# A decoder's two mixtures of experts with gate and input products in three fp16 passes

## The chip, the core and the metric

The kernel runs on one core of a Trainium2 chip. A core has a matrix engine (TensorE, in the trace PE, its weight loads PEld), VectorE (DVE), ScalarE (ACT), GpSimd (POOL), and SyncE (SP), which here only issues DMAs; each takes its instructions in order, and they meet at semaphores. The matrix engine reads from SBUF and writes to PSUM banks of 128 x 512 fp32. The metric is the device time of one execution in microseconds (us), median of several.

## The reference, cut to what matters

Two decoder layers over 1024 tokens of width 128. The change touches three of their six blocks.

```
# layer 0, mixture: 160 experts of inner width 64, 8 per token
probs  = sigmoid(x @ router.T + bias);  combine = 2.5 * top8(probs) / sum        # (T, 160)
h1     = silu(einsum('th,eih->eti', x, w_gate)) * combine.T[:, :, None]
out    = einsum('eti,ehi->th', h1, w_down) + silu(x @ w_gate_shared.T) @ w_down_shared.T
# layer 1, state space: in_proj, 4-tap convolution, silu, x_proj -> dt, B, C; softplus(dt);
#   16 states: h = exp(delta*A)*h + delta*B*u, y = sum C*h;  gate by silu(z), out_proj
# layer 1, mixture: 8 experts of inner width 512, 2 per token, at each of three linear maps
def moe_linear(x, router, w):  return sum_e top2_softmax(x @ router.T)[:, e] * (x @ w[e].T)
out = moe_linear(silu(moe_linear(x, rg, w_gate)) * moe_linear(x, ru, w_up), rd, w_down)
```

Inputs, weights and output are fp32.

## The kernel before

The six blocks are stages that run one after the other. Every instruction stands in an order written out by hand, engine by engine.

**First mixture** (moe0_stage, tiles f_, 971 to 1270 us). Two experts make a pair, so that their 2 x 64 inner columns fill 128 partitions: 80 pairs. The tokens are taken in two halves of 512; half 0 goes over all 80 pairs, then half 1. For each pair and half (an item) TensorE makes the gate product (L1765, weights `weights[:, pair, 0:P]` against 512 columns of xnT, fp32) into one of four banks, ScalarE applies silu (L1706), VectorE multiplies by the pair's combine rows (L1875, `spread`), and TensorE adds the down product (L1770, fp32) into out_ps. TensorE issues the gate product of item i+2 ahead of the down product of item i. `spread` is a ring of eight pairs in four groups of two: SP reads the combine rows from DRAM, each row repeated over 64 partitions, two DMAs of 256 KB for a group (L1631). In half 0 SP also loads the group's weights, one DMA of 256 KB (L1624); they stay in SBUF for half 1. SP refills a group four groups ahead, when VectorE has finished with it. Routing of half 1 is woven into the items of half 0 (front()).

**State space** (mamba_stage, tiles ssm_, banks m_b, 1271 to 1445 us). A prologue, a chain through all engines: normalize, transpose, in_proj, convolution on VectorE, silu, x_proj (L2036), dt (L2042), softplus on ScalarE and VectorE. Then 16 states: TensorE spreads a row of B over the partitions (L2051), VectorE multiplies (drive, L2150) and scans (L2156), GpSimd multiplies by C, TensorE sums (L2059).

**Second mixture** (moe1_stage, tiles g_, 2416 to 2626 us). Eight token tiles of 128. For each tile TensorE makes 16 products (L2942: 8 experts, gate and up; fp32, 128 x 512) into four banks in turn, and VectorE mixes each with the token's weight into a running sum (L3010, L3012); a product waits until the mix four before it has freed its bank. Then silu, the product of gate and up (L3019), four transposes, the third routing, two output products of four passes each (L2963), and VectorE combines the experts (L3037). The mixes of the next tile stand among these steps on VectorE, its products among the steps on TensorE. All input weights come in one DMA of 4 MB (L2890).

## Time and profile before

| | |
|---|---|
| runs | 2623.97, 2626.33, 2632.77 us; median 2626.33 |
| profiled execution | 2632.3 us, span 2630.4 us, mean granted clock 0.931 |
| busy | TensorE 2342.8 us (89%), VectorE 1966.3 (75%), ScalarE 1594.2 (61%) |
| gate products, first mixture (L1765) | 320 records, 168.1 us busy |
| down products, first mixture (L1770) | 320 records, 164.1 us busy |
| input products, second mixture (L2942) | 256 records, 118.2 us busy |
| scale by combine rows (L1875) | 160 instructions, 692 ns each |
| DMA of combine rows (L1631) | 160 issues of 256 KB |
| DMA of first mixture's weights (L1624) | 40 issues of 256 KB |

An fp32 product is recorded as two matmuls. Records overlap, since matmuls are pipelined; the distance from one start to the next is the time that one costs. The granted clock is 1.00 at 2.4 GHz and 0.50 at 1.2 GHz. A row of the timeline merges neighbours of one line (x2, x8); in brackets stands the idle time before it and what ended it.

### The profile page before, as it was taken

What the parts mean: (1) busy time and instruction counts of PE and PEld (TensorE: products, weight loads), DVE (VectorE), ACT (ScalarE), POOL (GpSimd) and SP (SyncE); (2) the same over time, 40 slices, a digit from 0 to 9 for tenths busy, and PEclk for the clock granted to TensorE, in tenths of its full rate; (3) what the DMA queues carried; (4) which work ended last, traced back from release to release, by engine and by line L of the source; (5) the groups of instructions that cost most, each with busy time, mean ns of one, the idle gap of its engine ahead of it and who ended that gap; (6) DMA issues with size and microseconds to landing.
All of it is one profiled execution on the core that took longest, in us unless ns stands there. A gap on an engine that the chain in (4) does not pass through costs nothing. (4 is left out here: it accounts for less than half of the span.)

```text
span 2630.4 us, 36895 instructions
## 1 busy us (share of the span) xinstructions
PE 2342.8 (89%) x12720; PEld 883.0 (34%) x12720; DVE 1966.3 (75%) x2808; ACT 1594.2 (61%) x1946; POOL 302.1 (11%) x334
## 2 busy tenths in 40 slices
PE   6888867999999979999678579999999999996998
PEld 3555511222222214444222223333333333332443
DVE  5676689999996114334599689999999999966775
ACT  5555477777777863333422578888888888753111
POOL 5666500000000000000056100000000000000000
PEclk8898856999999989999789779999999999997998
DMA  4454470221100129965111111112112111112000
GB/s 135 135 164 137 140 128 21 69 63 38 28 25 28 29 69 212 208 168 153 50 55 56 62 50 53 31 45 71 33 33 83 33 33 31 35 35 108 7 1 9
DMA packets 194589, 188.44 MB, mean 72 GB/s; under 512 B 18195, under 2 KB 155192, under 8 KB 193868
## 3 DMA queue, kind: packets, MB, share of 16 engines
q1 hardware_dynamic: 194132, 186.03, 26.0%
q8 instruction: 102, 1.67, 0.3%
q14 instruction: 67, 0.55, 0.1%
q10 hardware_dynamic: 288, 0.20, 0.0%
HBM read 144.60 MB, written 41.48 MB: 71 GB/s over the span
## 5 line engine op out<-in xcount | busy, mean ns | idle before, releaser
L2442 ACT ACTIVATE y_probs<-y_E,y_mask_bias 128x1024 f32<-128x1024 f32 x408 | 450.2, 1111 | 143.8 <-PE y_E L2537 142.1
L2754 DVE TENSOR_TENSOR y_acc<-y_acc,y_probs 128x1024 f32<-128x1024 f32 x400 | 487.0, 1217 | 41.4 <-ACT y_probs L2442 24.2
L1221 ACT ACTIVATE x_probs<-x_E 128x1024 f32<-128x1024 f32 x408 | 395.2, 1022 | 127.0 <-PE x_E L1282 126.4
L1406 DVE TENSOR_REDUCE x_maxima<-x_M 128x1 f32<-128x496 f32 x660 | 400.1, 667 | 20.9 <-PE x_M L1262 15.0
L2545 PE MATMUL y_O<-y_probs,y_values 128*64 128x512 f32 x1632 | 395.4, 605 | 0.0
L2533 PE MATMUL y_E<-y_q_parts,y_keys 64*128 64x512 f16 x2448 | 333.3, 378 | 1.4 <-ACT y_copied L2417 1.3
L2417 ACT ACTIVATE y_copied<-y_M 128x1024 bf16<-128x1024 f32 (+1 forms) x246 | 243.4, 989 | 30.1 <-PE y_M L2497 30.1
L1875 DVE TENSOR_TENSOR f_hidden<-f_act_out,f_spread 128x512 f32<-128x512 f32 x160 | 110.2, 692 | 177.4 <-ACT f_act_out L1706 144.4
L1296 PE MATMUL x_O<-x_probs,x_values 128*32 128x512 f32 x1632 | 217.8, 606 | 0.4 <-ACT x_probs L1221 0.4
L1706 ACT ACTIVATE f_act_out<-f_b 128x512 f32<-128x512 f32 x160 | 95.4, 597 | 189.0 <-PE f_b L1765 188.9
L1282 PE MATMUL x_E<-qs,x_keys 64*128 64x512 bf16 x1376 | 182.3, 377 | 4.9 <-ACT x_probs L1221 2.7
L1765 PE MATMUL f_b<-f_xnT,f_weights 128*128 128x512 f32 x320 | 168.1, 608 | 6.4 <-DMA f_weights<-f_w_in 6.2
L2702 DVE TENSOR_TENSOR y_running<-y_running,y_copied 128x3072 bf16<-128x3072 bf16 x96 | 162.2, 1690 | 11.0 <-ACT y_copied L2417 11.0
L2497 PE MATMUL y_M<-y_keys,y_q_parts 64*128 64x512 f16 (+1 forms) x736 | 142.3, 383 | 27.0 <-DVE y_maxima L2691 24.4
L2533 PEld LDWEIGHTS y_E<-y_q_parts,y_keys 64*128 64x128 f16 x2448 | 117.5, 95 | 142.0 <-ACT y_probs L2442 22.3
L2545 PEld LDWEIGHTS y_O<-y_probs,y_values 128*64 128x64 f32 x1632 | 99.2, 136 | 194.8 <-issue 140.7
L1770 PE MATMUL f_b<-f_hidden,f_weights 128*128 128x512 f32 x320 | 164.1, 595 | 0.0
L2537 PE MATMUL y_E<-y_m_rows,y_m_ones 64*128 64x512 f16 x816 | 155.5, 378 | 0.0
L2691 DVE TENSOR_REDUCE y_maxima<-y_M 128x2 f32<-128x1024 f32 (+1 forms) x104 | 123.3, 1186 | 36.1 <-PE y_M L2497 35.8
L1262 PE MATMUL x_M<-x_keys,qs 64*128 64x496 bf16 x596 | 117.9, 392 | 22.7 <-DVE x_maxima L1406 21.3
L2942 PE MATMUL g_b<-g_w_in,g_xnT 128*128 128x512 f32 x256 | 118.2, 607 | 4.8 <-DVE g_gate L3012 3.9
L2361 POOL TENSOR_TENSOR y_rstd<-y_var,mhalf 128x8 f32<-128x8 f32 x4 | 6.6, 1661 | 930.8 <-DVE y_var L2773 928.0
(493 smaller groups left out, 2949.5 us busy)
## 6 DMA issues: line engine op xcount, KB each, us to landing
f_spread<-comb_dram SPq DMA_DIRECT2D x160, 256.0 KB, 4.8
y_values<-v_dram SPq DMA_DIRECT2D x208, 128.0 KB, 2.2
v_dram<-a_v_out SPq DMA_DIRECT2D x26, 512.0 KB, 2.6
k_dram<-a_k_parts SPq DMA_DIRECT2D x26, 512.0 KB, 3.3
x_values<-v_dram SPq DMA_DIRECT2D x100, 128.0 KB, 2.2
f_weights<-f_w_in SPq DMA_DIRECT2D x40, 256.0 KB, 5.9
y_keys<-k_dram SPq DMA_DIRECT2D x36, 256.0 KB, 3.0
ssm_c_rows<-c_dram SPq DMA_DIRECT2D x16, 512.0 KB, 3.6
```

The source lines that it names most:

```text
L1221: nc.scalar.activation(probs[:, n % 2, 2 * g:2 * g + 2, :], psE[:, 2 * g:2 * g + 2, :], ACT.Exp).then_inc(exped, 1)
L1282: ins = T.matmul(psE[:, 2 * g + j, :], key_tile(2 * (u // 2) + g, low, t)[r, :], qs[r, u, low, g, :], start=(low == 0), stop=(low == 1))
L1296: ins = T.matmul(psO[32 * j:32 * j + 32, :], values[:, i, 32 * j:32 * j + 32], probs[:, n % 2, j, :], start=(t == 0), stop=(t == TILES0 - ...
L1406: V.tensor_reduce(maxima[:, 2 * j + h, qt, c:c + 1], psM[(2 * entry + j) % 3][:, 0:CHUNK0], AX.X, ALU.max).then_inc(max_done, 1)
L1765: T.matmul(gate_ps[i % ITEM_SLOTS][:], weights[:, pair, 0:P], xnT[:, HALF * h:HALF * h + HALF], start=True, stop=True).then_inc(gate_mm, 1)
L1770: T.matmul(out_ps[h][:], weights[:, pair, P:2 * P], hidden[:, i % ITEM_SLOTS, :], start=False, stop=last, skip_group_check=True).then_inc( ...
L2417: A(out[:, :, 0:width(c)], scores[:, :, 0:width(c)], ACT.Copy).then_inc(S["spare_copied"], 1)
L2442: A(probs[:, i, :], psE[:, 2 * (i % 2):2 * (i % 2) + 2, :].rearrange("p a b -> p (a b)"), ACT.Exp, bias=mask_bias[:, c * TILES_IN_TURN + i ...
L2533: T.matmul(psE[:, 2 * slot + j, :], keys[r, u // 2 % 2, key_part, tile * P:tile * P + P], q_parts[r, q_part, u // 2, q0:q0 + HALF], start= ...
L2545: ins = T.matmul(psO[u % 2][DH1 * j:DH1 * j + DH1, :], values[:, i, DH1 * j:DH1 * j + DH1], probs[:, i, 512 * j:512 * j + 512], start=Fals ...
L2702: V.tensor_tensor(so_far, so_far, new, ALU.max).then_inc(S["merged"], 1)
L2754: ins = V.tensor_tensor(acc[:, u % 2, :], acc[:, u % 2, :], probs[:, i, :], ALU.add)
```

## The change

**First mixture.** The gate product is made of three fp16 products into the same bank: upper half of the weights by upper half of the tokens, lower by upper, upper by lower. A value times a power of two, rounded to fp16, is the upper half; what the rounding left, again in fp16, the lower. ScalarE makes the upper halves (a scaled copy), VectorE the lower (scale and subtract), for weights a group of two pairs at a time, two groups ahead, among the items of half 0, and for tokens once a half. The down product stays fp32. Gate and down weights come in two DMAs of 128 KB where one of 256 KB was, six groups ahead where it was four; the gate weights go through a ring of eight staging slots. Silu takes the scale out. The loops of SP, ScalarE and VectorE over half 0 are written out where three of the ten turns were a loop.

**State space.** stay_busy() issues fp32 products of 512 columns whose result nobody reads: three before the transposes, two and three before the two halves of x_proj, one before dt, and fourteen, two at each of seven waits, between the first spread of B and the first state. The wait for z_done moves behind that spread.

**Second mixture.** The 16 products of a tile are each made of three fp16 products in the same way. ScalarE makes the upper halves of all 16 weight blocks and of both token halves, VectorE the lower: one token half and six blocks ahead of the routing, one block ahead of each of the first ten mixes of tile 0, and the second token half before the fifteenth. The 4 MB of weights come in eight DMAs. The factor of the scales goes into the mixing weights.

```diff
@@ first mixture (stage f_), weights on SP @@
-                def load_weights(g, pair):
-                    sp.dma_start(weights[:, bass.ds(pair, 2), :],
-                                 d.f0_w[bass.ds(pair, 2)].rearrange("a p n -> p a n")).then_inc(w_loaded[g], 16)
+                def load_weights(group):
+                    if group >= PAIRS // 2:
+                        return
+                    slot = group % STAGE_SLOTS
+                    if group >= STAGE_SLOTS:
+                        sp.wait_ge(w_split, group - STAGE_SLOTS + 1)
+                    sp.dma_start(staged[:, slot, :, :], d.f0_gate[group]).then_inc(w_loaded[slot], 16)
+                    sp.dma_start(down_w[:, 2 * group:2 * group + 2, :], d.f0_down[group]).then_inc(w_loaded[slot], 16)
...
-                            load_weights(g, first_pair + 2 * g)
+                            load_weights(n // 2 + g + GROUPS + AHEAD)
@@ first mixture, ScalarE: upper halves @@
+                def high_weights(group):
+                    if group < PAIRS // 2:
+                        slot = group % STAGE_SLOTS
+                        e.wait_ge(w_loaded[slot], 32 * (group // STAGE_SLOTS + 1))
+                        A(gate_w[:, 2 * group:2 * group + 2, 0, :], staged[:, slot, :, :], ACT.Copy, scale=W_SCALE0)\
+                            .then_inc(w_high, 1)
...
+                high_tokens(0)
+                for group in range(SPLIT_AHEAD):
+                    high_weights(group)
...
+                        if h == 0 and i % 2 == 0:
+                            high_weights((ITEMS * c + i) // 2 + SPLIT_AHEAD)
@@ first mixture, TensorE @@
-                        e.wait_ge(w_loaded[i // 2], loaded)
+                        e.wait_ge(w_split, pair // 2 + 1)
+                    if pair == 0:
+                        e.wait_ge(x_split, h + 1)
                     e.wait_ge(silu_done, n + (1 - ITEM_SLOTS + SILU0))
-                    T.matmul(gate_ps[i % ITEM_SLOTS][:], weights[:, pair, 0:P],
-                             xnT[:, HALF * h:HALF * h + HALF], start=True, stop=True).then_inc(gate_mm, 1)
+                    cols = slice(HALF * h, HALF * h + HALF)
+                    for w, part in ((0, 0), (1, 0), (0, 1)):
+                        ins = T.matmul(gate_ps[i % ITEM_SLOTS][:], gate_w[:, pair, w, :], x_parts[:, part, cols],
+                                       start=(w + part == 0), stop=(part == 1))
+                    ins.then_inc(gate_mm, 1)
@@ first mixture, VectorE: lower halves @@
+                def low_weights(group):
+                    if group < PAIRS // 2:
+                        e.wait_ge(w_high, group + 1)
+                        mine = gate_w[:, 2 * group:2 * group + 2, :, :]
+                        V.scalar_tensor_tensor(mine[:, :, 1, :], staged[:, group % STAGE_SLOTS, :, :], W_SCALE0,
+                                               mine[:, :, 0, :], ALU.mult, ALU.subtract).then_inc(w_split, 1)
@@ state-space stage (ssm_), TensorE @@
+                def stay_busy(bank, times):
+                    for _ in range(times):
+                        T.matmul(B[bank][:, 0:512], ident[:], in_proj[:], start=True, stop=True)
...
+                stay_busy(2, 3)
                 for h in range(2):
                     e.wait_ge(S["xn"], h + 1)
...
+                e.wait_ge(S["copied"], 1)
                 for j in range(CH):
+                    stay_busy(1, 2 + j)
                     e.wait_ge(S["silu_done"], j + 1)
...
-                e.wait_ge(S["z_done"], CH)
...
                 spread_b(0, 0)
+                e.wait_ge(S["copied"], 3)
+                for name, count, times in (("z_done", 2, 2), ("exped", 2, 2), ("lned", 2, 2), ("inved", 2, 2), ("soft", 1, 2),
+                                           ("soft", 2, 2), ("driven", 1, 2)):
+                    e.wait_ge(S[name], count)
+                    stay_busy(3, times)
@@ second mixture (stage g_) @@
-                sp.dma_start(w_in[:], d.f1_w_in).then_inc(S["w_in_loaded"], 16)
+                for ex in range(E1):
+                    sp.dma_start(w_in[:, ex, :, :], d.f1_w_in[:, ex]).then_inc(w_in_loaded[ex], 16)
...
-                        T.matmul(B[n % 4][:], xnT[:, P * t:P * t + P], w_in[:, n // 2, n % 2, :], start=True, stop=True)\
-                            .then_inc(S["in_mm"], 1)
+                        for part, w in ((0, 0), (0, 1), (1, 0)):
+                            ins = T.matmul(B[n % 4][:], x_parts[:, part, P * t:P * t + P], w_parts[:, n // 2, n % 2, w, :],
+                                           start=(part + w == 0), stop=(part == 1))
+                        ins.then_inc(S["in_mm"], 1)
...
+                low_tokens(0)
+                for n in range(6):
+                    low_weights(n)
                 e.wait_ge(S["load"], 16 * LOADS)
                 e.wait_ge(S["logits_sb"], 1)
...
-                mix(0, range(ITEMS))
+                for n in range(ITEMS):
+                    if n + 6 < ITEMS:
+                        low_weights(n + 6)
+                    if n == ITEMS - 2:
+                        low_tokens(1)
+                    mix(0, range(n, n + 1))
```

On TensorE, at the start of the first mixture, these rows stood before (f_xnT are the tokens, f_weights both weights, f_b the banks):

```order
L1765 MATMUL f_b<-f_xnT,f_weights 128x512 x2
L1719 MATMUL f_b<-f_xnT,f_shared_g 64x512
L1724 MATMUL f_b<-f_shared_h,f_shared_d 128x512
L1765 MATMUL f_b<-f_xnT,f_weights 128x512
L1770 MATMUL f_b<-f_hidden,f_weights 128x512
```

and these stand there now:

```order
L1799 MATMUL f_b<-f_x_parts,f_gate_w 128x512 x6
L1749 MATMUL f_b<-f_xnT,f_shared_g 64x512
L1754 MATMUL f_b<-f_shared_h,f_shared_d 128x512
L1799 MATMUL f_b<-f_x_parts,f_gate_w 128x512 x3
L1805 MATMUL f_b<-f_hidden,f_down_w 128x512
```

The order is the same; each gate product is three, of fp16 tiles, and so at each of the 160 items.

On VectorE, ahead of the first mixes of the second mixture, these rows stood before (L2873 to L2998 are the routing):

```order
L67 TENSOR_SCALAR g_xn<-x,g_moments,g_rstd 128x128 x8
L2873 MAX g_largest<-g_logits 128x8 x16
...
L2998 TENSOR_TENSOR g_comb<-g_one 128x128
L3010 TENSOR_SCALAR g_gate<-g_b,g_comb 128x512
L3010 TENSOR_SCALAR g_up<-g_b,g_comb 128x512
L3012 SCALAR_TENSOR_TENSOR g_gate<-g_b,g_comb,g_gate 128x512
```

and these stand there now:

```order
L67 TENSOR_SCALAR g_xn<-x,g_moments,g_rstd 128x128 x8
L3088 SCALAR_TENSOR_TENSOR g_x_parts<-g_xnT,g_x_parts 128x512
L3094 SCALAR_TENSOR_TENSOR g_w_parts<-g_w_in,g_w_parts 128x512 x6
L2947 MAX g_largest<-g_logits 128x8 x16
...
L3113 TENSOR_TENSOR g_comb<-g_one 128x128
L3094 SCALAR_TENSOR_TENSOR g_w_parts<-g_w_in,g_w_parts 128x512
L3125 TENSOR_SCALAR g_gate<-g_b,g_comb 128x512
L3094 SCALAR_TENSOR_TENSOR g_w_parts<-g_w_in,g_w_parts 128x512
L3125 TENSOR_SCALAR g_up<-g_b,g_comb 128x512
```

Seven instructions that make lower halves stand ahead of the routing, and one ahead of each of the first ten mixes.

## Rows read from the trace of the kernel before

**Rows 1.** Stretches: us, busy us (instructions) by engine, clock, DMA share, GB/s

```profile
1134.00:1267.00 133.00, 133.00 (x314) 58.96 (x313) 54.25 (x79) 46.01 (x78) 0.00 (x0) 1.00 0.53 142
```

**Rows 2.** Timeline, first mixture's second half: start, duration, engine, line, out<-in

```profile
1201.00 1.02 PE L1765 MATMUL f_b<-f_xnT,f_weights 128*128 128x512 f32 x2
...
1202.06 0.60 ACT L1706 ACTIVATE f_act_out<-f_b 128x512 f32<-128x512 f32 x1 [1.12 <-PE f_b L1765]
1202.78 0.69 DVE L1875 TENSOR_TENSOR f_hidden<-f_act_out,f_spread 128x512 f32<-128x512 f32 x1 [1.02 <-ACT f_act_out L1706]
...
1211.30 1.02 PE L1765 MATMUL f_b<-f_xnT,f_weights 128*128 128x512 f32 x2
```

**Rows 3.** Timeline of PE, 16-bit beside fp32 products in the second cross attention

```profile
1702.32 0.81 PE L2533 MATMUL y_E<-y_q_parts,y_keys 64*128 64x512 f16 x6
1702.97 0.38 PE L2537 MATMUL y_E<-y_m_rows,y_m_ones 64*128 64x512 f16 x2
...
1704.05 0.38 PE L2497 MATMUL y_M<-y_keys,y_q_parts 64*128 64x512 f16 x2
1704.36 1.94 PE L2545 MATMUL y_O<-y_probs,y_values 128*64 128x512 f32 x8
...
2092.80 0.41 PE L2559 MATMUL y_O<-y_zero 128*64 128x512 bf16 x2
2093.04 1.88 PE L2545 MATMUL y_O<-y_probs,y_values 128*64 128x512 f32 x8
```

**Rows 4.** Timeline of VectorE, first half: first and last of eight DMA waits

```profile
1096.42 1.34 DVE L1875 TENSOR_TENSOR f_hidden<-f_act_out,f_spread 128x512 f32<-128x512 f32 x2 [2.09 <-DMA f_spread<-comb_dram]
...
1123.80 1.48 DVE L1875 TENSOR_TENSOR f_hidden<-f_act_out,f_spread 128x512 f32<-128x512 f32 x2 [2.38 <-DMA f_spread<-comb_dram]
```

**Rows 5.** Stretches of the first half, columns as in rows 1

```profile
974.00:1127.00 153.00, 148.78 (x341) 63.47 (x342) 61.34 (x115) 52.53 (x86) 1.01 (x1) 0.96 1.01 212
1040.00:1080.00 40.00, 40.00 (x101) 18.13 (x100) 17.80 (x27) 14.22 (x24) 0.00 (x0) 1.00 1.03 221
1080.00:1120.00 40.00, 38.55 (x88) 15.89 (x87) 14.09 (x22) 12.54 (x21) 0.00 (x0) 1.00 1.09 199
```

**Rows 6.** Timeline of ScalarE, VectorE and PE in the second mixture

```profile
2425.18 0.60 ACT L2903 ACTIVATE g_xnT<-g_b 128x512 f32<-128x512 f32 x1 [0.26 <-PE g_b L2925]
2429.91 1.33 DVE L2873 MAX8 g_largest<-g_logits 128x8 f32<-128x8 f32 x16 [6.79 <-ACT g_logits L2905]
...
2436.03 0.75 DVE L3010 TENSOR_SCALAR g_gate<-g_b,g_comb 128x512 f32<-128x512 f32 x1
2436.70 0.74 DVE L3010 TENSOR_SCALAR g_up<-g_b,g_comb 128x512 f32<-128x512 f32 x1
...
2449.82 0.68 DVE L3019 TENSOR_TENSOR g_inter<-g_silu,g_up 128x512 f32<-128x512 f32 x1
...
2472.50 0.68 DVE L3019 TENSOR_TENSOR g_inter<-g_silu,g_up 128x512 f32<-128x512 f32 x1
...
2475.57 1.98 PE L2942 MATMUL g_b<-g_w_in,g_xnT 128*128 128x512 f32 x4 [0.65 <-DVE g_gate L3012]
```

**Rows 7.** Groups by line and shape: busy us, mean ns of one | idle

```profile
L2136 DVE SCALAR_TENSOR_TENSOR ssm_z<-ssm_z,ssm_delta 128x1024 f32<-128x1024 f32 x2 | 2.4, 1220 | 0.0
...
L430 ACT ACTIVATE a_k_parts<-a_T 128x512 f16<-128x512 f32 x52 | 30.9, 594 | 5.3 <-PE a_T L585 5.2
```

**Rows 8.** Stretches of the state-space prologue, columns as in rows 1

```profile
1291.00:1302.50 11.50, 6.11 (x14) 1.87 (x15) 4.92 (x5) 4.03 (x5) 0.00 (x0) 1.00 0.03 6
1302.50:1327.90 25.40, 6.32 (x8) 1.64 (x6) 20.32 (x17) 14.03 (x13) 0.00 (x0) 0.50 0.12 42
```

**Rows 9.** Timeline of VectorE in the first states of the scan

```profile
1331.85 2.29 DVE L2150 TENSOR_TENSOR ssm_drive<-ssm_du,m_b 128x2048 f32<-128x2048 f32 x1 [1.78 <-PE m_b L2051]
...
1339.88 2.29 DVE L2150 TENSOR_TENSOR ssm_drive<-ssm_du,m_b 128x2048 f32<-128x2048 f32 x1 [1.08 <-PE m_b L2051]
```

**Rows 10.** Page, part 5: weight loads of 16-bit products

```profile
L2533 PEld LDWEIGHTS y_E<-y_q_parts,y_keys 64*128 64x128 f16 x2448 | 117.5, 95 | 142.0 <-ACT y_probs L2442 22.3
```

More of the change, by code:

```diff
@@ L1574, in moe0_stage @@
         spread = sb("spread", [P, PAIRS_IN_TURN, HALF])
-        weights = sb("weights", [P, PAIRS, 256])
+        staged = sb("staged", [P, STAGE_SLOTS, 2, P])
+        gate_w, down_w = sb("gate_w", [P, PAIRS, 2, P], FP16), sb("down_w", [P, PAIRS, P])
+        x_parts = sb("x_parts", [P, 2, TOKENS], FP16)
         act_out = sb("act_out", [P, ITEM_SLOTS, 512])
@@ L1588, in moe0_stage @@
         GROUPS = PAIRS_IN_TURN // 2
-        w_loaded = [sem(f"w_loaded{g}") for g in range(GROUPS)]
+        w_loaded = [sem(f"w_loaded{g}") for g in range(STAGE_SLOTS)]
+        w_high, w_split, x_high, x_split = sem("w_high"), sem("w_split"), sem("x_high"), sem("x_split")
         c_loaded = [sem(f"c_loaded{g}") for g in range(GROUPS)]
@@ L1654, in _ @@
                 for g in range(1, GROUPS):
-                    load_weights(g, 2 * g)
+                    load_weights(g)
                     spread_rows(g, 2 * g, 0)
-                with sp.Fori(0, OPEN_TURNS) as c:
-                    load_turn(c * ITEMS, c * PAIRS_IN_TURN + PAIRS_IN_TURN, 0)
-                store_rows(1)
-                with sp.Fori(OPEN_TURNS, TURNS - 1) as c:
+                for g in range(AHEAD):
+                    load_weights(GROUPS + g)
+                for c in range(TURNS - 1):
+                    if c == STORE_TURN:
+                        store_rows(1)
                     load_turn(c * ITEMS, c * PAIRS_IN_TURN + PAIRS_IN_TURN, 0)
@@ L1705, in body @@
                         e.wait_ge(hidden_done, n + (i + 1 - ITEM_SLOTS + HID0))
-                        A(act_out[:, i % ITEM_SLOTS, :], gate_ps[i % ITEM_SLOTS][:], ACT.Silu).then_inc(silu_done, 1)
+                        A(act_out[:, i % ITEM_SLOTS, :], gate_ps[i % ITEM_SLOTS][:], ACT.Silu,
+                          scale=1.0 / (W_SCALE0 * X_SCALE0)).then_inc(silu_done, 1)
+                        if h == 0 and i % 2 == 0:
+                            high_weights((ITEMS * c + i) // 2 + SPLIT_AHEAD)
                         if h == 0 and isinstance(c, int) and ITEMS * c + i == 1:
                             shared(0)
-                        if pieces and ITEMS * c + i in ((2,) if h else (11, 20, 23, 39)):
+                        if pieces and ITEMS * c + i in ((2,) if h else (11, 15, 20, 23, 39)):
                             next(pieces)
@@ L1802, in _, with low_tokens @@
                 e.sem_inc(down_mm, DOWN0)
+                def low_weights(group):
[4 more added lines that the diff above has]
+                                               mine[:, :, 0, :], ALU.mult, ALU.subtract).then_inc(w_split, 1)
+                def low_tokens(h):
+                    e.wait_ge(x_high, h + 1)
+                    cols = slice(HALF * h, HALF * h + HALF)
+                    V.scalar_tensor_tensor(x_parts[:, 1, cols], xnT[:, cols], X_SCALE0, x_parts[:, 0, cols],
+                                           ALU.mult, ALU.subtract).then_inc(x_split, 1)
+                low_tokens(0)
+                for group in range(SPLIT_AHEAD):
+                    low_weights(group)
                 def front():
@@ L2828 @@
 E1, I1 = 8, 512
+W_SCALE1, X_SCALE1 = 2.0 ** 8, 2.0 ** 8
 IC = I1 // P
@@ L2858, in moe1_stage @@
         y = [sb(f"y{i}", [P, D]) for i in range(2)]
-        names = ("load w_in_loaded w_down_loaded dve to_pow from_pow xn tr xT_all logits_mm logits_sb diffed exped in_mm "
+        names = ("load w_high w_split x_high x_split w_down_loaded dve to_pow from_pow xn tr xT_all logits_mm logits_sb diffed exped in_mm "
                  "mixed silu_done inter_done i_tr iT rd_mm down_mm ddiff dexp y_done").split()
         S = {n: sem(n) for n in names}
+        w_in_loaded = [sem(f"w_in_loaded{ex}") for ex in range(E1)]
         LOADS = 3
@@ L2900, in _, with high_weights, high_tokens @@
                 A = nc.scalar.activation
+                def high_weights(ex):
+                    e.wait_ge(w_in_loaded[ex], 16)
+                    for g in range(2):
+                        A(w_parts[:, ex, g, 0, :], w_in[:, ex, g, :], ACT.Copy, scale=W_SCALE1).then_inc(S["w_high"], 1)
+                def high_tokens(j):
+                    cols = slice(512 * j, 512 * j + 512)
+                    e.wait_ge(S["xT_all"], j + 1)
+                    A(x_parts[:, 0, cols], xnT[:, cols], ACT.Copy, scale=X_SCALE1).then_inc(S["x_high"], 1)
                 for j in range(2):
@@ L2903, in _ @@
                     A(xnT[:, 512 * j:512 * j + 512], B[j][:], ACT.Copy).then_inc(S["xT_all"], 1)
+                high_tokens(0)
+                for ex in range(3):
+                    high_weights(ex)
                 e.wait_ge(S["logits_mm"], 1)
                 A(logits[:].rearrange("p a b -> p (a b)"), B[2][:, 0:2 * TILES * E1], ACT.Copy).then_inc(S["logits_sb"], 1)
+                high_weights(3)
                 e.wait_ge(S["diffed"], 1)
                 A(ediff[:], diff[:], ACT.Exp).then_inc(S["exped"], 1)
+                for ex in range(4, E1):
+                    high_weights(ex)
+                high_tokens(1)
                 for t in range(TILES):
```

62 lines of the change are left out of this document (45 added, 17 removed).

## The prediction

> **What bounds the kernel now.** I read the busy time by stretch first, then the timeline of TensorE where it is full, then what VectorE waits for where it is not. The first mixture's second half is TensorE's alone: 133.00 of 133.00 us busy at clock 1.00, the DMA engines at 0.53 of their time [rows 1]. Six items lie between 1201.00 and 1211.30 [rows 2], so one costs 10.30 / 6 = 1.717 us: two fp32 products of two passes, 1.717 / 4 = 0.429 us a pass. Silu (0.60) and the scaling (0.69) fit beside it and wait for TensorE.
>
> The first half looks the same from TensorE's busy time, but is not. Its last part waits for combine rows: eight waits of VectorE on the DMA of spread lie between 1096.42 and 1123.80 [rows 4], 27.38 / 7 = 3.91 us for a group of two pairs, where TensorE alone would take 2 x 1.717 = 3.43. A group brings 512 KB of combine rows and 256 KB of weights, 786,000 bytes; in 3.91 us that is 201 GB/s. The whole half ran at 212 GB/s with the DMA engines busy all the time (share 1.01), its early part at 221, its late part at 199 [rows 5]. Supply and TensorE were level: TensorE's own pace asks for 786 / 3.43 = 229 GB/s, and 40 groups at 3.43 us are 137 of the 153 us.
>
> In the second mixture TensorE and VectorE take turns: a tile lasts 2472.50 - 2449.82 = 22.7 us, VectorE mixes a product every 0.67 us (2436.03 to 2436.70), a product costs 0.858, and the one gap of TensorE in a tile is a wait of 0.65 us for a mix [rows 6].
>
> **The change part by part.** The profiled execution took 2632.3 us, 6 us above the median of 2626.33; the sum is made against it, and the difference carried over.
>
> *One product.* Six 16-bit passes of 512 columns on half the array start 0.65 us before what follows them, and the next pair steps the same way: 0.65 / 3 = 0.216 us a pass and pair of halves [rows 3]. I take 0.216 for a full 128 x 128 fp16 pass, half of the fp32 pass, so a gate product falls from 0.858 to 0.648. Changing kind of operand: from 16-bit to fp32 with the same shape, 0.24 us to the next start (2092.80 to 2093.04), 0.025 more than a pass; where the shape turns too, 0.31 (1704.05 to 1704.36), 0.10 more [rows 3]. The new item keeps one shape, so I charge 0.025: 0.858 + 0.648 + 0.025 = 1.53 us. Bounds: no charge, 1.507; a turn's charge both ways, 0.1 each, 1.71.
>
> *First mixture, second half.* The half has 80 items (133 / 1.717 = 77 of them in the stretch): 80 x -0.187 = -15.0 us. Nothing else comes last: silu 0.60 and the scaling 0.69 are under 1.53, and the 512 KB of combine rows for two items ask for 524 / 3.06 = 171 GB/s where 142 ran [rows 1] and 221 has been seen [rows 5].
>
> *First half.* TensorE would now need 3.06 us a group, which would ask for 257 GB/s; the bytes are the same. The stretch moved 212 x 153 = 32.4 MB. At its own mean rate nothing is gained: I take 0. At 221 throughout it takes 147 us (-6), at 199 it takes 163 (+10) [rows 5]; TensorE's own floor of 40 x 3.06 = 122 us (-31) would ask for a rate that no row has. The added work hides under that supply: ScalarE copies 40 blocks of 256 columns, and one of 512 in 16 bits took 594 ns [rows 7]; VectorE makes as many lower halves, by 1220 ns for 1024 columns about 0.35 us each [rows 7]. In 153 us VectorE has 61 us of work and ScalarE 53 [rows 5]; 14 to 15 more leave both far under the DMA. Without that cover one lower half in a group of 3.06 us still fits VectorE (2 x 0.69 + 0.35). Of queues: SP issues two weight DMAs for one, beside unchanged spread DMAs; a ScalarE copy that waits for its weights holds back the silu behind it, but weights come six groups ahead. Only at the start, where every buffer is empty, does silu of item 0 stand behind copies of the first groups; I count that inside the 0.
>
> *Second mixture.* A tile's products would be worth 16 x (0.858 - 0.655) = 3.2 us if TensorE were alone. But it already waits for VectorE once a tile [rows 6], and that gap grows where products outrun mixes at 0.67. By the order, seven products stand ahead of the gap's place and nine behind in VectorE's pace: 7 x 0.203 = 1.4, plus a little of the rest, 1.5 a tile. Seven tiles (the last steps of the last are unchanged): -10.5; bounds 0 and -22. Against it stands tile 0. VectorE makes seven lower halves ahead of the routing, each 1220 / 2 = 0.61 us [rows 7], from the end of ScalarE's first upper half (2425.18 + 0.60 for the token copy, 0.60 for its own [rows 6]): 2426.4 + 4.3 = 2430.7, where the routing began at 2429.91 with VectorE idle for 6.79 us ahead of it [rows 6]: +0.8. The mixes can then begin at 2436.03 + 0.8 = 2436.8. The first ten carry a lower half each, 10 x (0.61 + 0.67) = 12.8; six more mixes (4.0) and a token half (0.6) follow, which ends at 2454.2. With a silu of 0.6 and two hand-overs, an estimate of 1.4 together, the product of gate and up starts at 2455.6, where 2449.82 stood: +5.8. Bounds: +3 if lower halves run under waits for TensorE, +8. Sum for this stage: -10.5 + 5.8 = -4.7.
>
> *State space.* After 1302.5 TensorE runs at clock 0.50, with 6.32 busy of 25.4 us; before, it had 6.11 of 11.5 at 1.00 [rows 8]. In the first states VectorE then waits for the spread of B: 1.78 and 1.08 us [rows 9]. If the idle products hold the clock at 1.00, these waits go, and some of TensorE's 6.32 us ahead of them: -3 to -4, and VectorE, which scans, is last. If not, a product of 512 columns costs 1.72 us at the lower clock, and three ahead of the transposes, which everything behind them waits for, 5.1. Whether the few products suffice no row shows. I take -2, between -4 and +5, nearer to the gain because most of the idle products stand in waits for other engines.
>
> Sum: -15.0 + 0 - 4.7 - 2 = -21.7, so 2610.6 for the profiled execution and 2604.6 at the median: 2605 us.
>
> A rule speaks against this. In the rows a weight load of 95 ns stands beside each 16-bit product and does not lengthen the 0.216 us [rows 3, 10]; but these products use half of the array's rows. The Trainium skill, "TensorE: Matmul & The Clock Gate", section "The mechanism", states that a weight load overlaps a running matmul only where the two use different row groups. Full-height gate products would then each pay their load. The fp32 products of the second half use all rows and run at 0.429 us a pass with no gap [rows 2], which bears the rule out no further than that; no 16-bit full-height pass with a load of its own is in these rows. By the rule the result would be the fourth rival below, by the rows the sum stands.
>
> **The rivals.**
> - *The DMA keeps its early rate.* TensorE was busy 40.00 of 40 us at 221 GB/s [rows 5], so supply may have had more to give, and smaller weight DMAs may spread better. At 221 the first half loses 6 us more: 2599; at 230, 141 us, 2593. Against it: the share is 1.03 there already, and the late part fell to 199 with the engines no less busy.
> - *Kinds cost what turns cost.* If going to fp16 and back costs 0.1 us each way [rows 3], the item is 1.71 and the second half gains 1 us. In the second mixture products and output passes alternate behind the first tiles; paying there too, it keeps perhaps 2 of its 4.7. With -2 for the state space that is -5: 2621, no change that can be told. Against it: the fp32 product behind the bf16 one started after 0.24 us.
> - *The idle products delay.* They stand ahead of the transposes at the lower clock and do not raise it: +5 for -2, 2612. This also covers the case that they don't do what they are for.
> - *The weight loads are exposed* (the slower side). Place: each fp16 pass of gate and input products, on TensorE. If a pass pays p us for its load, the second half pays 80 x 3 x p and the second mixture 7 tiles x 21 x p, together 387 x p. At 0.095 [rows 10] that is +37: -21.7 + 37 = +15, 2641. It decides from p = 21.7 / 387 = 0.056 us. For it: nothing in the rows shows a 16-bit pass on the whole array with a load of its own. Against it: a pass of 0.216 us is longer than the load, and the fp32 loads vanish beside their passes [rows 2].
>
> **How the numbers follow.** Forecast 54%; early rate 17%; costly kinds 10%; exposed loads 10%; delaying idle products 9%. About 0.3% (8 us) can be told from no change. Forecast, early rate and idle products are faster by more than that: 80%; costly kinds within it: 10%; exposed loads slower: 10%. The range: the forecast's own is 2593 to 2617 (first half -12 to +8, tile 0 and the idle products +-3). The early rate at 230 and a second mixture at its better bound reach 2590, the delaying idle products with a slow first half 2621; left out are exposed loads and the costly kinds where they cost more.
>
> **What would show it.** In the changed profile's second half six items should lie 9.2 us apart, not 10.3, with fp16 starts 0.216 apart; at 0.31 the loads are exposed. In the first half TensorE should have gaps and VectorE's waits on spread should begin much earlier than 1096, at 3.4 to 3.9 us a group. The product of gate and up should come at about 2455 less what was gained before, and then every 21.2 us. In the state space the clock after the idle products and the two waits of rows 9 tell which case it is. A scaling or silu that TensorE waits for in the second half, or a first half longer than 163 us, would make the prediction wrong.

## The result, and the profile after

The changed kernel takes 2592.88 us (median of four, 2588.11 to 2595.96) against 2629.55 for the one before: a ratio of 0.9868, 95% interval [0.985, 0.9887], or 34.7 us less (30 to 39 by the interval; the two medians differ by 36.7). The forecast was 2605, 21.3 us below the median then shown. The direction and most of the mechanisms held; all four terms of the sum were too small, and the time came out at the low end of the range.

The profiled executions differ by 2630.4 - 2594.2 = 36.2 us of span. Cut at instructions that both kernels have, the starts in the two traces give (the second mixture ends with its last add):

| stretch | before, us | after, us | difference | forecast |
|---|---|---|---|---|
| first mixture, last add of the cross attention to 80th scaling | 158.45 | 154.60 | -3.9 | 0 |
| 81st to 160th scaling | 136.00 | 119.34 | -16.7 | -15.0 |
| whole first mixture, to the first statistics of the state space | 301.54 | 280.89 | -20.7 | -15.0 |
| state space | 180.89 | 176.58 | -4.3 | -2 |
| second mixture | 209.10 | 199.80 | -9.3 | -4.7 |

That is -34.3. The other 1.9 us lie in stages whose instructions are the same in both (3.2 less ahead of the first mixture, 1.2 more in the second cross attention): one execution differs from another by as much there.

**First mixture, second half.** The stretch of the changed profile that answers to [rows 1]: TensorE is still busy throughout at clock 1.00, VectorE and ScalarE stay below half, the DMA engines at 0.60, 168 GB/s.

```profile
1122.00:1240.00 118.00, 118.00 (x396) 53.08 (x396) 54.70 (x80) 47.07 (x79) 0.00 (x0) 1.00 0.60 168
```

TensorE's timeline there, answering to [rows 2]: from the gate product at 1136.88 to the one six items later at 1145.92.

```profile
1136.88 0.81 PE L1799 MATMUL f_b<-f_x_parts,f_gate_w 128*128 128x512 f16 x3
1137.53 1.02 PE L1805 MATMUL f_b<-f_hidden,f_down_w 128*128 128x512 f32 x2
1138.39 0.81 PE L1799 MATMUL f_b<-f_x_parts,f_gate_w 128*128 128x512 f16 x3
...
1145.92 0.81 PE L1799 MATMUL f_b<-f_x_parts,f_gate_w 128*128 128x512 f16 x3
```

Six items take 9.04 us, 1.507 each. Three fp16 passes take 1137.53 - 1136.88 = 0.65 (0.216 a pass), two fp32 passes 0.86. Going to fp32 and back costs nothing: the 0.025 that was charged is not there. Nor is a charge for weight loads, which the group of loads shows beside it (480 loads of 99 ns):

```profile
L1799 PEld LDWEIGHTS f_b<-f_x_parts,f_gate_w 128*128 128x128 f16 x480 | 47.1, 99 | 116.6 <-issue 88.1 <-DVE f_gate_w L1843 8.5 <-ACT f_act_out L1733 1.5
```

**First mixture, first half.** ScalarE's timeline at the start. The second and the third copy of a group's weights each wait over 4 us for their DMA, and the silu that stands behind a copy waits too: the two silus are 5.1 us apart.

```profile
976.76 0.42 ACT L1692 ACTIVATE f_gate_w<-f_staged 128x256 f16<-128x256 f32 x1 [4.26 <-DMA f_down_w<-f_down_in]
977.08 0.58 ACT L1733 ACTIVATE f_act_out<-f_b 128x512 f32<-128x512 f32 x1
981.87 0.42 ACT L1692 ACTIVATE f_gate_w<-f_staged 128x256 f16<-128x256 f32 x1 [4.20 <-DMA f_down_w<-f_down_in]
982.19 0.58 ACT L1733 ACTIVATE f_act_out<-f_b 128x512 f32<-128x512 f32 x1
```

So the second scaling starts 16.0 us after the last add, where it was 9.0, and the third 20.8 where it was 15.9. All of that is made up later: at the twentieth scaling 0.7 us of it are left, and at the fortieth the changed kernel is 3.3 ahead. VectorE now waits for combine rows from 1041 on, 74 us after the last add, where the waits of [rows 4] began 126 us after it. The waits come 3.70 us apart, between the 3.4 and 3.9 that the prediction had named; the first of them and one of the last:

```profile
1041.26 0.69 DVE L1929 TENSOR_TENSOR f_hidden<-f_act_out,f_spread 128x512 f32<-128x512 f32 x1 [1.17 <-DMA f_spread<-comb_dram]
...
1115.16 0.69 DVE L1929 TENSOR_TENSOR f_hidden<-f_act_out,f_spread 128x512 f32<-128x512 f32 x1 [1.48 <-DMA f_spread<-comb_dram]
```

The stretch as a whole, beside the first line of [rows 5]: TensorE idle for 15.4 us, the DMA engines busy all the time at 218 GB/s where 212 stood.

```profile
971.00:1117.00 146.00, 130.64 (x410) 53.98 (x411) 72.94 (x154) 65.57 (x125) 1.01 (x1) 0.94 1.04 218
```

**State space.** The input products, first in the kernel before and then in the changed one (columns as in rows 1): they run at clock 1.00 where 0.59 stood.

```profile
1281.40:1286.40 5.00, 5.00 (x9) 2.23 (x8) 2.59 (x7) 1.69 (x2) 0.00 (x0) 0.59 0.00 0
```

```profile
1257.70:1261.00 3.30, 3.26 (x8) 1.61 (x9) 2.40 (x6) 1.50 (x2) 0.00 (x0) 1.00 0.03 7
```

Three more stretches of the changed kernel: convolution to the first spread of B, softplus, and the first state. The first now runs at clock 1.00 (0.90 in the kernel before, from 1287.0 to 1306.4), the second at 0.81 where [rows 8] had 0.50.

```profile
1261.00:1278.30 17.30, 16.81 (x38) 5.63 (x37) 9.71 (x9) 8.65 (x8) 0.00 (x0) 1.00 0.07 14
1278.30:1296.40 18.10, 15.90 (x29) 6.06 (x28) 15.27 (x15) 12.09 (x11) 0.00 (x0) 0.81 0.15 48
1296.40:1305.50 9.10, 7.22 (x11) 2.15 (x10) 6.75 (x3) 2.24 (x2) 4.15 (x2) 0.68 0.00 0
```

But the two waits of VectorE that were to go, [rows 9], are still there:

```profile
1305.53 2.29 DVE L2220 TENSOR_TENSOR ssm_drive<-ssm_du,m_b 128x2048 f32<-128x2048 f32 x1 [2.18 <-PE m_b L2116]
...
1313.30 2.29 DVE L2220 TENSOR_TENSOR ssm_drive<-ssm_du,m_b 128x2048 f32<-128x2048 f32 x1 [0.82 <-PE m_b L2116]
```

**Second mixture.** VectorE at the start and at the first products of gate and up, answering to [rows 6]: routing at 2403.53, the first mix at 2410.11, and mixes and lower halves in turn.

```profile
2399.92 3.69 DVE L3094 SCALAR_TENSOR_TENSOR g_w_parts<-g_w_in,g_w_parts 128x512 f16<-128x512 f32 x6
2403.53 1.18 DVE L2947 MAX8 g_largest<-g_logits 128x8 f32<-128x8 f32 x16
...
2410.11 0.74 DVE L3125 TENSOR_SCALAR g_gate<-g_b,g_comb 128x512 f32<-128x512 f32 x1
2410.77 0.68 DVE L3094 SCALAR_TENSOR_TENSOR g_w_parts<-g_w_in,g_w_parts 128x512 f16<-128x512 f32 x1
2411.37 0.74 DVE L3125 TENSOR_SCALAR g_up<-g_b,g_comb 128x512 f32<-128x512 f32 x1
...
2427.96 0.70 DVE L3134 TENSOR_TENSOR g_inter<-g_silu,g_up 128x512 f32<-128x512 f32 x1
...
2447.87 0.68 DVE L3134 TENSOR_TENSOR g_inter<-g_silu,g_up 128x512 f32<-128x512 f32 x1
...
2468.95 0.68 DVE L3134 TENSOR_TENSOR g_inter<-g_silu,g_up 128x512 f32<-128x512 f32 x1
```

A tile lasts 2468.95 - 2447.87 = 21.1 us. TensorE waits for VectorE three times in it (0.48, 0.43, 1.03), once before (0.65):

```profile
2446.03 2.14 PE L3039 MATMUL g_b<-g_w_parts,g_x_parts 128*128 128x512 f16 x9 [0.48 <-DVE g_gate L3127]
2448.60 0.66 PE L3047 MATMUL g_b<-ident_sb,g_inter 128*128 128x128 f32 x4 [0.43 <-DVE g_inter L3134]
2449.10 0.81 PE L3039 MATMUL g_b<-g_w_parts,g_x_parts 128*128 128x512 f16 x3
2450.94 1.48 PE L3039 MATMUL g_b<-g_w_parts,g_x_parts 128*128 128x512 f16 x6 [1.03 <-DVE g_gate L3127]
```

### The profile page after: what moved, and what is told of

Its sections match the earlier page's. It is cut to its first block and busy times, and to the rows that moved or that the text cites. A ratio compares the mean times of both kernels' runs of the same rounds, so it can differ in the third digit from the quotient of the medians.

```text
span 2594.2 us, 37475 instructions
## 1 busy us (share of the span) xinstructions
PE 2304.3 (89%) x13054; PEld 858.1 (33%) x13054; DVE 1987.8 (77%) x2868; ACT 1618.2 (62%) x2006; POOL 301.8 (12%) x334
## 5 line engine op out<-in xcount | busy, mean ns | idle before, releaser
L1805 PE MATMUL f_b<-f_hidden,f_down_w 128*128 128x512 f32 x320 | 165.8, 601 | 7.8 <-DVE f_hidden L1929 7.7
L1262 PE MATMUL x_M<-x_keys,qs 64*128 64x496 bf16 x596 | 117.9, 392 | 22.7 <-DVE x_maxima L1406 21.3
L1799 PE MATMUL f_b<-f_x_parts,f_gate_w 128*128 128x512 f16 x480 | 131.9, 385 | 6.3 <-DVE f_gate_w L1843 6.3
L3039 PE MATMUL g_b<-g_w_parts,g_x_parts 128*128 128x512 f16 x384 | 94.0, 392 | 16.1 <-DVE g_gate L3127 10.4
```

What stands on the lines that cost most here:

```text
L1805: T.matmul(out_ps[h][:], down_w[:, pair, :], hidden[:, i % ITEM_SLOTS, :], start=False, stop=last, skip_group_check=True).then_inc(down_mm, 1)
```

## The experiments

Stage times below are worked out from the starts in each run's trace, as in the first table; "80th" is the time from the last add of the cross attention to the 80th scaling, "next 79" from the 81st scaling to the 160th, "state space to last drive" from that stage's first statistics to its last drive product, "first gate x up" from the first statistics of the second mixture to tile 0's product of gate and up, "seven tiles" from there to the last tile's. The first four kernels of the experiments ran on one chip, the next three on another, the last on a third.

| kernel | 80th | next 79 | state space to last drive | first gate x up | seven tiles |
|---|---|---|---|---|---|
| before | 158.45 | 136.00 | 160.5 | 33.13 | 160.0 |
| changed | 154.60 | 119.34 | 157.8 | 38.28 | 146.7 |
| first mixture alone | 143.74 | 119.34 | 162.9 | 32.97 | 160.0 |
| state space alone | 150.46 | 136.00 | 158.2 | 33.13 | 160.0 |
| second mixture alone | 150.73 | 136.00 | 161.7 | 38.30 | 146.6 |
| weight DMAs alone | 152.86 | 136.00 | 162.9 | 32.99 | 160.0 |
| half the rows | 140.30 | 119.34 | 158.3 | 38.30 | 146.7 |
| other idle products | 150.61 | 119.34 | 161.3 | 32.41 | 146.6 |
| early weights, late combining | 141.93 | 119.34 | 157.9 | 37.66 | 136.2 |
| GpSimd halves | 143.57 | 119.34 | 158.6 | 40.08 | 136.2 |

**The three parts by themselves.** Each is the kernel before with one stage function (and its layout of weights) from the changed one, as in the diff above.

> The kernel before with the first mixture's part of the change alone. Theory (the three parts do not lean on each other): its stage takes what it takes in the changed kernel, 20.6 us less than before: the first half about 4 us (DMA-bound, a fuller queue), the second 16.7 us (80 items of 1.506 instead of 1.717 us). About 2609 us at the median, ratio 0.992. Rival (the parts share something, the clock or the DMA queue): another gain than 20.6 in this stage, or one outside it.

> The kernel before with the idle products of the state-space stage alone. Theory: the stage falls by 4.3 us as in the changed kernel, through input products and dt at the clock of 1.00 (1.6 and 1.2 us) and the end of the stage (1.6 us), not through the two waits of VectorE for the spread of B, which stay near 2.2 and 0.8 us. About 2625 us, ratio 0.998. Rival (the end of the stage belongs to the clock's own course and not to the idle products): 2.7 us or less.

> The kernel before with the second mixture's part alone. Theory: 9.3 us less in its stage: the first tile's product of gate and up 5.1 us later, the seven distances to the last one 13.3 us shorter together, the rest behind the last 1.2 us shorter. About 2620 us, ratio 0.9965. Rival: if part of it came from the clock that earlier stages leave, the tile distances are above 21.1 us.

Measured: 0.9909 [0.9884, 0.9935], 0.9979 [0.9963, 0.9995] and 0.9966 [0.9948, 0.9984], together 1.5% less, where the whole change gives 1.3% with an interval of 1.1 to 1.5. The second mixture repeats its 9.3 us to a tenth. The state space does too up to its last drive product: 158.2 us, against 160.5 to 162.9 in the four kernels without idle products. Its end is another matter: the 1.6 us there come and go with kernels that do not touch the stage (18.8 us from the last drive to the next stage in three of them, 20.4 in the kernel before and in this run), so the theory was wrong to count them.

The first mixture did not repeat: its first half took 143.7 us, not 154.6. Nor did the unchanged first half of the other two, 150.5 and 150.7 where the kernel before had shown 158.45. The stretch from the third scaling to the 80th of the kernel with the state space alone (first half as before) and of the one with the first mixture alone:

```profile
981.09:1117.97 136.88, 136.88 (x333) 60.87 (x332) 60.35 (x109) 50.73 (x83) 1.01 (x1) 1.00 1.01 227
```

```profile
986.58:1111.24 124.66, 124.12 (x411) 53.78 (x409) 71.69 (x147) 62.39 (x121) 1.01 (x1) 1.00 1.06 236
```

With the DMA engines as busy as in [rows 5], 227 and 236 GB/s ran where 212 had. In the old first half TensorE was then busy throughout: the transfers were not in its way, although the DMA share of 1.01 looks full. So 227 GB/s is what TensorE's pace asked for; no limit of the DMA shows in it. On this chip the change gives 143.7 - 150.6 = -6.9 us here: 12.3 us less from the third scaling on (137.0 to 124.7), of which the later start takes 5.4.

**The weight transfers alone.**

```diff
-  sp.dma_start(weights[:, bass.ds(pair, 2), :], d.f0_w[...])          # 256 KB, four groups ahead
+  sp.dma_start(gate_w[:, 2 * group:2 * group + 2, :], d.f0_gate[group])   # fp32, no split, six ahead
+  sp.dma_start(down_w[:, 2 * group:2 * group + 2, :], d.f0_down[group])
```

> The kernel before with the first mixture's new weight transfers alone: gate and down weights in two DMAs of 128 KB each, six groups ahead, loops written out; gate products stay one fp32 product, nothing is split. From the last add of the cross attention to the 80th scaling the kernel before took 158.4 us, the changed one 154.6. Theory (the shorter products free the ring of combine rows earlier, which keeps the DMA queue full): with TensorE as before the transfers alone give less than 1.5 us of these 3.8, 157 to 159 us. Rival (the transfers ahead are what fills the queue): 154 to 155.5 us here too. The second half stays at 1.717 us an item under both.

Measured: 0.9991 [0.9975, 1.0007], 152.9 us to the 80th scaling, against 150.5 and 150.7 on the same chip. Both bounds of the expectation were made with another execution's rate and neither fits as written; beside kernels on the same chip the transfers alone gain nothing, so the 6.9 us above come with the shorter products. Whether the transfers fill the queue better the run can't show, since TensorE was the limit in it from the third scaling to the 80th:

```profile
982.99:1120.02 137.03, 137.03 (x333) 61.10 (x332) 60.30 (x109) 50.75 (x83) 1.01 (x1) 1.00 0.97 222
```

**Half the combine rows; idle products apart; no lower halves.**

```diff
 # half the rows (first half, from the second turn of the ring on)
-  for e in range(2):
+  for e in range(1 if h == 0 and pair >= PAIRS_IN_TURN else 2):
 # half the rows: the fourteen idle products are left out; other idle products: the nine ahead of them are
 # other idle products, second mixture: no low_weights(); the second pass reads the upper half
-  w_parts[:, n // 2, n % 2, w, :]
+  w_parts[:, n // 2, n % 2, 0, :]
```

> The changed kernel with two edits in stages that follow each other. First mixture, first half: from the second turn of the ring on only one of the two DMAs of combine rows is issued (the other 64 partitions keep older rows, so the output is not the reference's). From the last add of the cross attention to the 80th scaling it took 154.6 us in the changed kernel's profile and 143.7 with this mixture alone. Theory (the DMA queues carry the first half): with 524 KB for a group where 786 KB were, TensorE's 1.506 us an item is the limit, some 16 us of start and 78 items, 133 to 140 us. Rival (the half waits for hand-overs, not for bytes): 143 us or more. State space: without the fourteen idle products behind the first spread of B. Theory (the gain comes from the nine in front of the transposes, x_proj and dt): up to the last drive product the stage keeps its 157.8 us within 0.5, VectorE's first two gaps between drive products are 8.7 and 8.0 us as before the change where 9.1 and 7.8 stand now. Rival (the fourteen carry the gain): 159 us or more.

> The changed kernel with two edits. State space: only the fourteen idle products, without the nine ahead of the transposes, x_proj and dt. Theory (the nine give the gain): up to the last drive product 160.5 to 163 us, as in kernels without idle products, where the changed kernel has 157.8; rival: below 159. Second mixture: VectorE makes no lower halves of the weights; the second pass of each product takes the upper half once more (so the output is not the reference's, and TensorE's work is the same). Theory (the lower halves stand on the path of tile 0): the first product of gate and up starts 31.5 to 32.5 us into the stage where the changed kernel has 38.3 and the one before 33.1, later tiles stay 21.1 us apart. Rival (they lie beside waits for TensorE): 36 us or more. The first mixture is that of the changed kernel: from the last add of the cross attention to the 80th scaling 154.6 us there and 143.7 with that mixture alone; theory (the DMA rate differs from one execution to the next): anywhere between 143 and 156, in step with the GB/s of that stretch.

Measured: with half the rows 140.3 us, 0.3 above the top of the first theory's range and well under the rival's 143. This is what remains when transfers are out of the way:

```profile
972.00:1108.00 136.00, 130.31 (x429) 57.58 (x428) 76.58 (x156) 65.97 (x128) 1.01 (x1) 0.96 0.62 174
```

So the transfers cost the changed first half 14.3 us in its own profile, 10.3 in the kernel with other idle products, and 3.4 with the first mixture alone. One size for this wait does not exist. The first mixture is the same code in these three; where VectorE waits for combine rows, its waits come 3.70, 3.63 and 3.30 us apart, a group of 786,000 bytes each.

Idle products: without the fourteen the stage reaches its last drive at 158.3 us, 0.5 more than the changed kernel; without the nine at 161.3. That is the difference between kernels with and without idle products (157.8 to 158.6, and 160.5 to 162.9), so the nine carry the gain. What the fourteen do is not the same each time: with the nine there VectorE's first two gaps between drive products are 9.1 and 7.8 us, without the fourteen 8.8 and 8.1, but with the fourteen alone 8.0 and 7.0. In that run the clock came back to 1.00 before the second drive product; in the changed kernel TensorE was at the lower level from 1299.6 to 1309.8 despite them. The nine do not decide it: the last kernel below has all twenty-three, and there too the gaps are 8.0 and 7.0 and the clock is back at 1.00 before the second drive product. What decides this is not shown.

No lower halves of weights: the first product of gate and up comes at 32.4 us into the stage instead of 38.3, and the later tiles stay 21.1 apart. The kernel before had 33.1, so VectorE's lower halves of the weights account for all that tile 0 lost.

**Early weights, late combining.** The first four groups' weights are loaded during the last unit of the cross attention; in the second mixture the experts of a tile are combined behind the sixth mix of the next, four lower halves stand ahead of the token half, and ScalarE makes the first two experts' upper halves ahead of its token copies.

```diff
+  if u == UNITS - 1 and t in range(12, 28, 4):            # cross attention, SP
+      sp.dma_start(k.f_gate_first[:, group, :, :], d.f0_gate[group])
+      sp.dma_start(k.f_down_first[:, 2 * group:2 * group + 2, :], d.f0_down[group])
 # second mixture, VectorE
-  if 0 < t < TILES - 1: combine(t - 1, 1)
-  mix(t + 1, range(2, 10))
+  mix(t + 1, range(2, 6))
+  if 0 < t < TILES - 1: combine(t - 1, 0); combine(t - 1, 1)
+  mix(t + 1, range(6, 10))
   ...
-  combine(t, 0)
+  if t >= TILES - 2: combine(t, 0)
```

> The changed kernel with what the theories point to. First mixture: the weights of the first four groups come during the last unit of the cross attention, 1 MB of the first half's transfers earlier. Theory (bytes are the limit): at 212 to 230 GB/s 4.3 to 4.9 us less in the first half, the second scaling at 9 us after the last add where 16 stood; rival (the start does not count, since the queue is full during it, and the ring is the limit): under 2 us less. Second mixture: VectorE combines a tile's experts behind the sixth mix of the next tile rather than ahead of the third and fifteenth mix, and four lower halves stand ahead of the token half. Theory (TensorE's waits of 0.47, 0.43 and 1.03 us in a tile come from the mixes that stand behind the combining): tiles 19.6 to 20.2 us apart where 21.1 stood, tile 0 up to 2.4 us earlier. Rival (VectorE is the limit of a tile): 20.8 us or more. In all 2578 to 2586 us if both theories hold, ratio to the kernel before 0.980 to 0.983.

Measured: 2575.3 us, 0.9808 [0.9782, 0.9835]: with the next kernel the fastest of all. The second scaling starts at 8.5 us, the 80th at 141.9, 8.7 less than in the kernel with other idle products on the same chip, whose first mixture is the changed one. That is more than its 1 MB explains (4.3 to 4.9 us). Of the 8.7 us 6.9 are there at the tenth scaling and no more at the fortieth: they come from the start that is no longer stalled. The other 1.7 come where VectorE waits for combine rows, and whether the bytes or the rate of that execution made them is not shown. Tiles are 19.35 us apart, below the theory's range. TensorE's wait for a mix is gone from the tile; what is left is one for the combining itself:

```profile
2436.51 3.67 PE L3081 MATMUL g_b<-g_w_down,g_interT 128*128 128x512 f32 x8 [0.66 <-DVE g_y L3174]
```

Tile 0 came only 0.6 us earlier: ten lower halves still stand among its mixes.

**Lower halves on GpSimd.**

```diff
+  for n in range(8, ITEMS):                                # GpSimd; ScalarE has scaled w_in before
+      nc.gpsimd.tensor_tensor(parts[:, 1, :], w_in[:, n // 2, n % 2, :], parts[:, 0, :], ALU.subtract)
-  if n + 6 < ITEMS: low_weights(n + 6)                     # VectorE
+  if n + 6 < 8: low_weights(n + 6)
```

> The kernel with early weights and later combining, and in tile 0 of the second mixture the lower halves of the last eight weight blocks come from GpSimd (ScalarE scales them first, one copy more for each block), so that VectorE makes two beside its mixes where it made ten. Theory (VectorE's lower halves are what tile 0 waits for, 0.63 us each): the first product of gate and up starts 32.5 to 33.5 us into the stage where 37.7 stood, tiles 19.35 us apart as there; 4 to 5 us less in all, about 2571 us. Rival (GpSimd's subtractions are slower than the mixes or slow VectorE down beside them): 35 us or more, with TensorE waiting for GpSimd or mixes longer than 0.66 us apart.

Measured: 0.9803 [0.9772, 0.9834], no different from the kernel it is built on; the product of gate and up comes at 40.1 us, 2.4 later. The rival holds, but not through the mixes. The eight subtractions run from 2396.55 to 2405.68,

```profile
2396.55 9.13 POOL L2995 TENSOR_TENSOR g_w_parts<-g_w_in,g_w_parts 128x512 f16<-128x512 f32 x8 [12.26 <-ACT g_w_parts L3011]
...
2396.88 0.91 DVE L2973 CAST g_wheref<-g_where 128x128 f32<-128x128 uint32 x1
2397.82 1.03 DVE L2975 TENSOR_SCALAR g_p<-g_ediff 128x16 f32<-128x16 f32 x1
2398.88 0.25 DVE L2976 RECIPROCAL g_p<-g_p 128x16 f32<-128x16 f32 x1
...
2399.99 2.36 DVE L3143 TENSOR_TENSOR g_one<-g_iota,g_wheref 128x128 f32<-128x128 f32 x2
```

and beside them VectorE's routing slows down. The same instructions in the kernel without GpSimd's part:

```profile
2390.28 4.25 ACT L2999 ACTIVATE g_w_parts<-g_w_in 128x512 f16<-128x512 f32 x8
...
2392.34 0.23 DVE L2972 CAST g_wheref<-g_where 128x128 f32<-128x128 uint32 x1
2392.60 0.17 DVE L2974 TENSOR_SCALAR g_p<-g_ediff 128x16 f32<-128x16 f32 x1
2392.81 0.25 DVE L2975 RECIPROCAL g_p<-g_p 128x16 f32<-128x16 f32 x1
...
2393.30 0.49 DVE L3128 TENSOR_TENSOR g_one<-g_iota,g_wheref 128x128 f32<-128x128 f32 x2
```

ScalarE copied weight blocks beside the routing in this kernel too (2390.28 to 2394.53), so ScalarE's copies do not explain it. From the conversion to the first lower half behind the routing it was 2.35 us (2392.34 to 2394.69) and is 9.0 (2396.88 to 2405.86). Without these 6.6 us the product of gate and up would come at about 33.5, the upper end of the theory's range. The mixes that follow, when GpSimd is done, run at 0.66 again.

## Why the prediction was right in direction, and where its terms failed

**Second half: right, and 1.7 us too small.** The item was to fall from 1.717 to 1.53 and fell to 1.507. The pass of 0.216 us, taken from products on half of the array, held for the full array. The charge of 0.025 us for changing kind was the term that failed: in the changed item the fp32 product starts 0.216 us after the last fp16 pass. In the row that it was read from both products use 128 rows and 64 columns; where its 0.24 us come from is not shown.

**Exposed weight loads: excluded.** The rival needed 0.056 us a pass and the trace leaves nothing: 0.216 with a load of 99 ns each. The rule of the Trainium skill, "TensorE: Matmul & The Clock Gate", section "The mechanism", that a load overlaps a running matmul only in another row group, does not agree with this trace, in which loads for all 128 rows vanish beside passes on all 128 rows. The section itself also names a background weight buffer; which of the two a load uses here no row shows.

**First half: the step "at its own mean rate nothing is gained" failed.** It took the 212 GB/s of one execution for what the DMA can give. For most of that stretch TensorE set the rate itself: it was busy for 148.78 of the 153 us, and in three later runs with the old gate products for all of the time from the third scaling on, at 222 to 227 GB/s. A DMA share of 1.01 does not tell the two cases apart. The prediction's first rival, the early rate, was nearer on this term: it gave -6 at 221 GB/s, and the change gains 3.9 us between the two first profiles and 6.9 between kernels on one chip. Neither figure can be sharper than the executions: the old first half took 150.5 to 158.45 us, the changed one 143.7 to 154.6, and the runs do not part the execution from the chip that it ran on. The floor was 122 us; with half of the rows the half still takes 140.3, since the start (14.4 us to the second scaling) and what else TensorE does there are not in 40 x 3.06. The stall at the start, "counted inside the 0", was 7.0 us at the second scaling and 4.9 at the third; the shorter items made it up before VectorE began to wait for combine rows.

**Second mixture: both terms named, the gain mis-sized.** Tile 0 came 5.15 us later, +5.8 forecast, by the mechanism that was named; without lower halves it is gone. The seven distances gave -13.2 where -10.5 stood. The step "seven products ahead of the gap's place, nine in VectorE's pace" was too strict: TensorE's busy time in a tile fell by 3.06 us (22.20 to 19.14) and its waits grew from 0.65 to 0.48 + 0.43 + 1.03 = 1.94, so 1.3 us a tile were lost and not 1.7. They were a matter of order and not of VectorE's load: with combining moved a tile falls to 19.35. The last 1.2 us, behind the last tile, were not forecast; as that tail also differs by 0.6 us between kernels that do not touch it (15.37 and 15.99), how much of it belongs to the change is open. The 0.655 us that the sum used for a product has no source in the rows; three passes are 0.648.

**State space: the size in the range, the step wrong.** The waits of 1.78 and 1.08 us were to go, and are 2.18 and 0.82: the products did not hold the clock at 1.00 through the first state, where it was 0.68. In the two kernels in which it was back at 1.00 before the second drive product, the first two gaps fell from 8.7 and 8.0 us to 8.0 and 7.0, so the link from the clock to these waits is borne out. In the changed kernel the gain is ahead of them: input products at clock 1.00 bring the convolution 1.6 us earlier, and dt at 1.00 shortens the second of its two steps by 1.2 in these profiles. The other 1.6 of the 4.3 us, at the end of the stage, are not shown to be the change's. Most idle products stand in waits, as the prediction said; but those that pay are the nine that stand ahead of work.

In sum all four terms were off to the same side: -16.7 - 3.9 - 9.3 - 4.3 = -34.2 for -21.7. The time is near what the prediction gave for its first rival (2593 to 2599), but not for that reason alone: of the 12.5 us that the sum lacked 3.9 lie in the first half, and 4.6 in the second mixture.

## What to carry to other kernels

Where a stretch stands at the limit of its transfers, one profile gives one draw of their rate, and where it does not, the rate is the engine's own pace, even at a DMA share of 1.01: look at the same stretch in several executions, or cut the bytes once, before a gain of the engine behind it is set to nothing. A faster producer moves waits to where its consumer's order has something else in between; look there first, since moving that work (here the combining of experts) was worth nearly as much as the faster products in that stage. Preparing operands costs most where the engine that prepares them is the one waited for, and giving it to an engine that slows the first one down is no way out.

## What the runs showed of the hardware that was not expected

- GpSimd's subtraction of two SBUF tiles slows most of VectorE's instructions beside it to four to six times (0.23 to 0.91 us, 0.17 to 1.03, 0.49 to 2.36 for two), a reciprocal not at all (0.25 both times). The Trainium skill, "SBUF — State Buffer", section "Who interferes with whom", states that a VectorE instruction with two SBUF inputs contends with a GpSimd instruction that reads SBUF, as does one in a 2-port mode (a cast or tensor_scalar can be in one), and that whoever issues first has the shared ports for its whole instruction. The run agrees: one subtraction takes 9.13 / 8 = 1.14 us, a little more than these three slowed instructions grew by (0.68 to 0.94 each).
- The same first mixture had its groups of combine rows and weights, 786,000 bytes each, 3.30, 3.63 and 3.70 us apart in three executions while VectorE waited for them. Why is open; the three ran in different kernels, at least two of them on different chips.
- fp16 and fp32 products of the same shape follow each other without a charge: 0.216 us from the last fp16 pass to the fp32 one, 0.43 from the last fp32 pass.
